# Causal scores and values of a retention layer in halves of 64 keys, two heads on the partitions

## The reference, cut to what matters

```
x = x + 0.5 * ffn(layernorm(x))
x = x + retention(layernorm(x))
x = x + 0.5 * ffn(layernorm(x))

retention(x):                      # 16 heads of 16 channels
    q, k, v = split(x @ w_qkv);  q, k = rotate(q), rotate(k)
    scores = (q @ k^T) * 16**-0.5 * mask      # mask[t, s] = gamma_h**(t - s) for t >= s, else 0
    y = group_norm(scores @ v) * gn_weight + gn_bias
    return (silu(x @ w_g) * y) @ w_proj
```

## Time and profile before

| | |
|---|---|
| time, median of 3 runs | 159.17 us (159.16 to 159.94) |
| time of the profiled execution | 159.67 us |
| its span | 157.3 us |
| TensorE busy | 151.1 us (96%) |
| VectorE busy | 124.5 us (79%) |
| ScalarE busy | 77.8 us (49%) |
| GpSimd busy | 68.4 us (43%) |

### The profile page before, as it was taken

How to read it: one execution, slowest core, us unless ns; L and a number is a source line. 1 busy time by engine, 2 the same in 40 slices (tenths; PEclk the granted TensorE clock), 3 DMA queues, 4 the chain that set the end, 5 groups by cost and what they waited for, 6 DMA issues and landing times.

```text
span 157.3 us, 3410 instructions
## 1 busy us (share of the span) xinstructions
PE 151.1 (96%) x1199; PEld 117.4 (75%) x1199; DVE 124.5 (79%) x271; ACT 77.8 (49%) x179; POOL 68.4 (43%) x76
## 2 busy tenths in 40 slices
PE   5998999999999999999999999999999999999992
PEld 2375688788979568957786878668688887888991
DVE  0897999998897769579696969896944999656684
ACT  3476997687113150615435272637565648473310
POOL 3446344774973400183655647186699420000000
PEclk9999999999999999999999999999999999999999
DMA  4999402804000000000000000000000000001103
GB/s 125 328 368 307 158 0 76 328 5 133 0 0 4 0 0 4 0 0 0 6 0 4 2 4 0 4 0 2 4 2 0 0 4 0 0 0 63 38 33 133
DMA packets 7007, 8.40 MB, mean 53 GB/s; under 512 B 448, under 2 KB 5712, under 8 KB 6992
## 3 DMA queue, kind: packets, MB, share of 16 engines
q1 hardware_dynamic: 6816, 8.13, 15.4%
q10 hardware_dynamic: 176, 0.07, 0.3%
HBM read 7.15 MB, written 1.05 MB: 52 GB/s over the span
## 4 chain that ended last, share of the span: by engine, by line
PE 61%; POOL 13%; DVE 10%; issue 9%; DMA 2%; ACT 1%; POOLq 0%; DVEq 0%; ACTq 0%
PE bank L1157 26%; PE bank L1185 13%; POOL grstd L338 7%; PE bank L1213 5%; PE bank L1283 3%; DVE sc L798 3%; PE bank L1338 2%; DMA xt<-in_L_attn_x 2%; PE bank L1259 2%; DVE stats L694 2%; POOL rstd L316 2%; POOL state L346 2%; PE bank L1227 2%; PE bank L1230 2%; POOL ve L314 1%
## 5 line engine op out<-in xcount | busy, mean ns | idle before, releaser
L1157 PE MATMUL bank<-hh,up_r 128*128 128x512 f32 x92 | 25.5, 400 | 0.1
L1157 PE MATMUL bank<-hh,gate_r 128*128 128x512 f32 x92 | 25.6, 401 | 0.0
L1185 PE MATMUL bank<-down_r,fhi 128*128 128x256 f32 x96 | 24.1, 289 | 0.0
L338 POOL TENSOR_TENSOR grstd<-gve,neg_half 128x16 f32<-128x16 f32 x8 | 23.5, 2932 | 0.7
L1185 PE MATMUL bank<-down_r,flo 128*128 128x256 f32 x96 | 23.4, 282 | 0.0
L453 ACT ACTIVATE gact<-bank,vec 128x512 f32<-128x512 f32 x24 | 16.3, 685 | 9.1 <-PE bank L1157 8.3
L798 DVE TENSOR_TENSOR sc<-bank,msk 128x512 f32<-128x512 f32 x32 | 20.6, 680 | 0.0
L1157 PEld LDWEIGHTS bank<-hh,up_r 128*128 128x128 f32 x92 | 16.8, 188 | 4.3 <-issue 0.5
L461 ACT ACTIVATE fhi<-fuse 128x512 fp32r<-128x512 f32 x24 | 14.6, 625 | 10.8 <-DVE fuse L741 10.8
L1157 PEld LDWEIGHTS bank<-hh,gate_r 128*128 128x128 f32 x92 | 16.9, 188 | 4.0 <-ACT gate_r L402 0.4
L1185 PEld LDWEIGHTS bank<-down_r,fhi 128*128 128x128 f32 x96 | 18.1, 188 | 0.7 <-issue 0.2
(11 more groups left out here) (90 smaller groups left out, 284.5 us busy)
## 6 DMA issues: line engine op xcount, KB each, us to landing
raw<-in_rotation SPq DMA_DIRECT2D x1, 1536.0 KB, 7.8
out<-xt SPq DMA_DIRECT2D x8, 128.0 KB, 1.7
raw<-in_L_ffn_down_w SPq DMA_DIRECT2D x2, 384.0 KB, 7.3
wqkv<-in_L_attn_w_qkv SPq DMA_DIRECT2D x1, 768.0 KB, 9.6
xt<-in_L_attn_x SPq DMA_DIRECT2D x2, 256.0 KB, 3.6
xt<-in_L_attn_x SPq DMA_DIRECT2D x1, 512.0 KB, 5.4
raw<-in_rotation SPq DMA_DIRECT2D x1, 512.0 KB, 3.4
raw<-in_L_ffn_gate_w SPq DMA_DIRECT2D x1, 384.0 KB, 6.0
```

Source lines behind the costliest of these rows:

```text
L338: pool.tensor_tensor(grstd[:, c % 2], gve[:, :], neg_half[:, :], ALU.pow).then_inc(grstd_done, 1)
L1157: mm = pe.matmul(dst[:, :], wr[m][:, k * I + i * P:k * I + (i + 1) * P], half[:, k, g % NG, :], start=(k == 0 and half is hhi), stop=(k == ...
L1185: mm = pe.matmul(downs[d][:, 0:C], half[:, g % NG, i, t * P:(t + 1) * P], wr["down"][:, i * C:(i + 1) * C], start=(i == 0 and half is fhi) ...
```

## The change

The causal half is used. For the first 64 keys of a chunk all 128 queries matter, for the last 64 keys only the last 64 queries. Two heads by 64 keys now stand on the 128 partitions.

- `scores`: the stationary operand is `kM` (32 rows; two heads by 64 keys, 128 columns, the other head's rows 0), the moving one is `qT` (128 queries for the first half of the keys, 64 for the second): 16 matmuls for a chunk in place of 8, of 192 columns for a pair of heads in place of 256.
- `mask_scores` works on 384 columns in place of 512.
- `values`: the contraction is over two heads by 64 keys, with `v2` block-diagonal (32 columns, both heads); 16 matmuls as before, 8 of them of 64 columns in place of 128.
- `copy_qk` no longer makes `kT` and `qM` (three copies), but `kM` (two copies with a scale); `qT` is as before.
- `copy_v` makes `v_own` (all of v, for `update_state`) and then four copies of 64 partitions by 8 by 16 into `v2`, before it signals that v is ready.

```diff
@@ masks
-        np.eye(P), p[:, None] <= p[None, :], p[:, None] // D == p[None, :] // D,
+        np.eye(P), s[:, None] <= np.arange(P)[None, :], s[:, None] <= np.arange(P // 2)[None, :],
+        p[:, None] // D == p[None, :] // D,
@@ tiles
-        qM = sb("qM", [P, KC, 2, P])
-        kT = sb("kT", [P, KC, P])
-        v2 = sb("v2", [P, 2, H, 2 * D])
-        sc = sb("sc", [P, HG, KC, 2, P])
+        kM = sb("kM", [P, KC, 2, 2, HP])
+        v_own = sb("v_own", [P, 2, H // 2, 2 * D])
+        v2 = sb("v2", [P, 2, 2, H // 2, 2 * D])
+        sc = sb("sc", [P, HG, KC, SP])
@@ copy_v
-                nc.scalar.activation(v_own[c % 2], b_vg[:, 0:C].rearrange("p (a e w) -> p a e w", e=2, w=D),
-                                     ACT.Copy).then_inc(v_done, 1)
+                nc.scalar.activation(v_own[:, c % 2], b_vg[:, 0:C].rearrange("p (a w) -> p a w", w=2 * D), ACT.Copy)
+                v_src = b_vg[:, 0:C].rearrange("p (a e w) -> p a e w", e=2, w=D)
+                for half in range(2):
+                    for m in range(2):
+                        last = nc.scalar.activation(v2[m * HP:(m + 1) * HP, c % 2, half, :, m * D:(m + 1) * D],
+                                                    v_src[half * HP:(half + 1) * HP, :, m], ACT.Copy)
+                last.then_inc(v_done, 1)
@@ copy_qk
-                nc.scalar.activation(kT[:, :, :], k_src, ACT.Copy)
                 for m in range(2):
-                    last = nc.scalar.activation(qM[:, :, m, :], q_src, ACT.Copy, scale=msk[:, 3 * P + m:3 * P + m + 1])
+                    last = nc.scalar.activation(kM[:, :, :, m, :], k_src.rearrange("p k (a s) -> p k a s", a=2), ACT.Copy,
+                                                scale=msk[:, 2 * P + SP + m:2 * P + SP + m + 1])
@@ mask_scores
-                dve.tensor_tensor(sc[:, r].rearrange("p k m t -> p (k m) t"),
-                                  b_sc[r][:, :].rearrange("p (g t) -> p g t", t=P),
-                                  causal.unsqueeze(1).to_broadcast([P, 2 * KC, P]), ALU.mult).then_inc(sc_masked, 1)
+                dve.tensor_tensor(sc[:, r], b_sc[r][:, 0:KC * SP].rearrange("p (k t) -> p k t", t=SP),
+                                  causal.unsqueeze(1).to_broadcast([P, KC, SP]), ALU.mult).then_inc(sc_masked, 1)
@@ scores
                 for k in range(KC):
-                    for r in range(HG):
-                        at = slice(r * 2 * D, (r + 1) * 2 * D)
-                        mm = pe.matmul(b_sc[r][:, k * C:(k + 1) * C], kT[at, k, :],
-                                       qM[at, k].rearrange("p m t -> p (m t)"), start=True, stop=True)
+                    for half in range(2):
+                        for r in range(HG):
+                            at = slice(r * 2 * D, (r + 1) * 2 * D)
+                            mm = pe.matmul(b_sc[r][:, k * SP + half * P:k * SP + P + half * HP],
+                                           kM[at, k, half].rearrange("p m s -> p (m s)"), qT[at, c % 2, k, half * HP:P],
+                                           start=True, stop=True)
@@ values
                 for k in range(KC):
-                    for r in range(HG):
-                        if k == 0:
-                            pe.wait_ge(sc_masked, c * HG + r + 1)
-                        for m in range(2):
-                            hd = (k * HG + r) * 2 + m
-                            mm = pe.matmul(b_y[r * 2 * D:(r + 1) * 2 * D, k * P:(k + 1) * P], v2[:, c % 2, hd, :],
-                                           sc[:, r, k, m, :], start=(c == 0 and m == 0), stop=(m == 1), skip_group_check=True)
+                    for half in range(2):
+                        for r in range(HG):
+                            if k == 0 and half == 0:
+                                pe.wait_ge(sc_masked, c * HG + r + 1)
+                            mm = pe.matmul(b_y[r * 2 * D:(r + 1) * 2 * D, k * P + half * HP:(k + 1) * P],
+                                           v2[:, c % 2, half, k * HG + r, :], sc[:, r, k, half * P:P + half * HP],
+                                           start=(c == 0 and half == 0), stop=(half == 1), skip_group_check=True)
@@ update_state
-                                       rot[:, c % 2, C + a * 2 * D:C + (a + 1) * 2 * D], v_own[c % 2][:, a],
+                                       rot[:, c % 2, C + a * 2 * D:C + (a + 1) * 2 * D], v_own[:, c % 2, a],
```

More of the change, by code:

```diff
@@ L38 @@
 TH = 4
+HP = P // 2
+SP = P + HP
 GT = TH * P
@@ L117, in masks @@
     p = np.arange(P)
+    s = p % (P // 2)
     return np.concatenate([
-        np.eye(P), p[:, None] <= p[None, :], p[:, None] // D == p[None, :] // D,
+        np.eye(P), s[:, None] <= np.arange(P)[None, :], s[:, None] <= np.arange(P // 2)[None, :],
+        p[:, None] // D == p[None, :] // D,
         (p[:, None] // D) % 2 == np.arange(2)[None, :],
@@ L142, in macaron @@
         wp = sb("wp", [P, KC, C])
-        msk = sb("msk", [P, 3 * P + 2])
+        msk = sb("msk", [P, 2 * P + SP + 2])
         rows = sb("rows", [2 * NI + 2 * KC, P])
@@ L188, in macaron @@
         early = 2 * KC * I // (2 * C)
-        ident, causal, own = msk[:, 0:P], msk[:, P:2 * P], msk[:, 2 * P:3 * P]
+        ident, causal, own = msk[:, 0:P], msk[:, P:P + SP], msk[:, P + SP:2 * P + SP]
         gate_col, up_col = vec[:, 0:NI], vec[:, NI:2 * NI]
         gnw_col, gnb_col = vec[:, 2 * NI:2 * NI + KC], vec[:, 2 * NI + KC:2 * NI + 2 * KC]
-        v_own = [v2[:, b].rearrange("p (a e) w -> p a (e w)", e=2).rearrange("p a (u w) -> p a u w", w=D)[:, :, 0::3]
-                 for b in range(2)]
         def piece(base, q):
@@ L348, in _ @@
             pool.memset(neg_half[:, :], -0.5).then_inc(const_done, 1)
-            pool.memset(v2[:, :, :, :], 0.0).then_inc(v_zero, 1)
+            pool.memset(v2[:, :, :, :, :], 0.0).then_inc(v_zero, 1)
             pool.wait_ge(const_done, 1)
@@ L1342, in _ @@
             pe.wait_ge(v_zero, 1)
-            zeros = v2[:, 0].rearrange("p h w -> p (h w)")
+            zeros = v2[:, 0].rearrange("p a h w -> p (a h w)")
             for _ in range(WARM_UP):
```

## The result

Five runs of each kernel on one chip gave a median of 160.54 us with the change (160.21 to 160.78) and 159.57 us before (159.16 to 159.94): a ratio of 1.0064, 95% interval 1.0038 to 1.0090. The change makes the kernel about 1 us slower. The forecast was 158.0 us, faster, with a range of 157.0 to 159.4; the result lies above the range.

What follows compares the result with a forecast made beforehand. Two tied limits were taken as the bound: TensorE's list and a loop through GpSimd, 8.42 us a chunk. Shifts of -0.65, +0.16, -0.08, -0.30, 0 and -0.35 summed to -1.2 us, a median of 158.0; range 157.0 to 159.4.

Steps and rivals of the forecast that it cites:

- the price of ScalarE's four copies in `copy_v`: ScalarE ahead of `affine`: 0.15 to 0.16 us per plain 128-column copy, 0.63 for four; bounds for one 0.13 to 0.35.
- the ScalarE rival: ScalarE in `copy_v`: dearer copies cancel the gain, 159.8 us at 0.27 a copy; decides from 0.20 on; chance 0.17.
- ScalarE's copies lengthen the loop: Chunks 2, 3, 4 and ahead of `project_qk(1)`: copies at 0.27 cost 4 x 0.45 more, 159.8 us; chance 0.17.
- `values`: TensorE, each chunk: four rounds of 128 columns and four of 64, 0.66 us in place of 0.88, gain 0.22.
- `scores`: TensorE, each chunk: eight rounds limited by weight loads of 0.11 us, gain 0.05; bounds 0.20 gained to 0.74 lost.
- The rival in which loads do not hide: TensorE in `scores`: loads wait for matmuls in their own rows, 1.54 us a chunk for 0.86; 162.5 us; chance 0.10.
- Masks: VectorE: 128 fewer columns save 0.13 us an instruction, 4.2 us in all, most of which covers nothing.
- The two limits: Chunk loop: TensorE's own list, which the change shortens, ties at 8.42 us with a loop through GpSimd, which it doesn't.
- TensorE is the only limit: Whole kernel: the tie is a coincidence and gn has room, so 8 x 0.27 = 2.2 us go, 157.0; chance 0.13.
- ScalarE's two losses (0.16 and 0.06): Terms of the sum: +0.16 us for late ga in chunk 2, +0.06 for h of chunk 1 behind chunk 0's copies.
- term of +0.16 for a late ga in chunk 2: Chunk 2's turn of y: TensorE has no lead yet and ga is late by the added copies, +0.16 us.
- the gain is absorbed: From 72.98 on: gn, ga and the powers keep their times, as after any small shift; 158.9 us; chance 0.10.

Runs made afterwards that it cites:

- e1: Kernel before plus groups of four ScalarE copies of several forms behind its last work; plain groups took 0.76 to 0.79 us, the change's own four 1.17.
- e6: Changed kernel with its four copies all from and to partitions 0 to 63; 157.60 us against 159.13 before, ratio 0.9896.
- e5: Kernel before with the group norm's power on GpSimd replaced by a multiply; 158.77 us against 159.13, ratio 0.9971.
- e7: Changed kernel with copies made late from SBUF, and the group norm's power replaced by a multiply; 156.64 us against 159.13 before, ratio 0.9842.
- e4: Changed kernel with the four copies taken from v_own in SBUF, behind copy_y, with their own semaphore; 157.31 us against 159.36 before, ratio 0.9883.
- e3: Changed kernel with the four copies into v2 taken out; 157.38 us against 159.36 before, ratio 0.9889.
- e9: Kernel before plus groups of four copies behind ScalarE's last work; 1.10, 1.13, 1.10 us with alternating start partitions, 0.77 where only partition number changes.

## Why the prediction was wrong, step by step

**The step that failed** is the price of ScalarE's four copies in `copy_v`: "0.15 to 0.16 for a plain copy of 128 columns: 0.63 us for four". It is right for neighbours with the same start partition (0.157 in e1) and wrong for these four, which start 0.27 to 0.29 apart and take 1.13 us. I had worked it out from copies that all use all 128 partitions; no copy of the trace before uses fewer. The rival's remark, "64 partitions with a stride of 16 in 32 appear nowhere in the trace", named the wrong suspects: e1 shows that neither 64 partitions nor the stride costs anything. The bounds that I gave, 0.13 to 0.35, held the value. The range did not use the upper one: it stopped "half way into the ScalarE rival". With the four at the forecast spacing (e6), the kernel is 1.5 us faster and not 1 us slower, so this one term turned the sign.

**What the size did** went by the mechanism as forecast: ga comes too late for the turn of y inside the closed loop. The table's shifts less the forecast ones are +0.40 at turned norm 0, +0.89 at 1, +1.37 at 2, +1.89 at 3 and at 4, and +2.31 at 7. So each of the steps to turned norms 0, 1, 2 and 3 lost 0.40 to 0.52 against its term, the step from 3 to 4 nothing, and the last one 0.42: about the price error of four copies, 4 x 0.125 = 0.5, five times over. The rival "ScalarE's copies lengthen the loop" had 159.8 us for a copy of 0.27, +0.6 on the median; measured is +1.0 for 0.28. It counted four places and missed the fifth, the turn of y of chunk 5 behind `affine(4)`, before and changed:

```profile
109.31 0.44 PE L1315 MATMUL bank<-msk,yT 128*128 128x128 f32 x2
...
110.67 0.41 PE L1322 MATMUL bank<-msk,yT 128*128 128x128 f32 x2 [0.32 <-issue]
```

From turned norm 4 it is 2.00 us to this turn before and 2.34 in the changed kernel: 0.34 arises right there.

**`values`**: forecast 0.22 us a chunk, measured 0.26 (1.11 to 0.85). A round of 64 columns costs 0.056 (one starts at 85.37, the next at 85.43), as extrapolated; four such rounds give 0.21. The other 0.05 was not in the sum: the four strips of a round now start within 0.02 us, where they had come to start up to 0.07 apart.

**`scores`**: forecast 0.05 of gain with weight loads as the limit (0.86 - 0.88 + 0.055 is 0.035, so 0.05 was the rounder figure and not the sum's), measured 0.02 (1.07 to 1.05 from the first matmul to the next function's). The loads of the eight rounds start 0.11 apart, whether the round moves 128 columns or 64. The rival in which loads do not hide fell: it had 1.54 us for a chunk. (The Trainium skill, "TensorE: Matmul & The Clock Gate", Part 3, The mechanism, says that a load overlaps a matmul in flight only where the row group differs, though it also names a background weight buffer that a load may go into ahead. This trace disagrees with the first by itself: the loads of two rounds on the same four strips run from 85.92 to 86.23, while the first round's matmuls run from 85.93 to 86.32, and the 32 instructions end within 1.12 us.)

**Masks**: forecast 0.13 us each, measured 0.132, and 4.2 us of VectorE in all. No run tests by itself how much of that reaches the time.

**The two limits**: that there are two, close to each other, was right, but they do not tie at 8.42 us. TensorE's list takes 8.42 before and 8.14 after (e5 and e7), the loop some 8.28 (e4, where TensorE waits for gn), so there is 0.14 for a shorter list to gain where I had put 0.08. For a version whose copies are out of the way the rival "TensorE is the only limit" (157.0, a gain of 2.2) is a little nearer than my sum, which without ScalarE's two losses (0.16 and 0.06) comes to 1.4: turned norm 7 gains 1.73 in e3 and 1.94 in e4. That sum was thus 0.3 to 0.5 us too small. Its term of +0.16 for a late ga in chunk 2 is more than its own numbers give (0.63 less 0.52 of slack is 0.11); e6 shows 0.12. The prediction's other rival, "the gain is absorbed" (158.9), had no row behind it, and e6 shows the gain arriving.

**How sure it was.** 0.13 for slower than 160.0 was too little: the one operation whose form appeared nowhere in the trace stood in front of a wait with 0.5 us of slack, and a price well inside its bounds turned the sign.

## What to carry to other kernels

Price an added instruction by its spacing beside its real neighbours, not by its length alone, and where no row shows such neighbours let the upper bound carry the range. Ask of each added instruction on an idle engine what stands behind it in that engine's list and how much slack that has: ScalarE was idle half of the time, and four small copies at the wrong place turned 1.2% faster into 0.6% slower. A chain that nearly ties with the busiest engine takes part of the gain (0.49 us here), but less than a late operand did (2.5 us).

## What was unexpected in the hardware

Two neighbouring ScalarE copies of 128 columns from PSUM start 0.157 us apart if their start partitions are the same, and 0.28 us apart if that of the source or of the destination changes between them by 64, or both change by 32 (e9; 32 on one side alone was not run). Crossing the partitions (source from 64, destination from 0) costs nothing by itself, nor do 64 partitions in place of 128, nor a stride (e1, four copies in 0.76 to 0.79 us each time). A copy from SBUF instead of PSUM is slower: the change's four in e4 last 1.25 us against 1.11.
